# Two-layer cross-attention: stacked operands and row maxima sent to the score matmuls in another order and further ahead

## What is computed

```python
q = hidden @ Wq + bq; k = ctx @ Wk + bk; v = ctx @ Wv + bv      # 256 -> 256, 64, 64
scores = einsum('bkgld,bksd->bkgls', q, k) / sqrt(8) + mask     # 8 key heads, groups of 4
out = einsum('bkgls,bksd->bkgld', softmax(scores), v)
x = out @ Wo + bo + hidden
hidden = (x - mean) * rsqrt(var + 1e-6) * gamma + beta          # input of the second layer
```

## Time and profile before

| | us |
|---|---|
| median of 3 runs | 390.87 |
| range of the runs | 389.21 to 392.48 |
| profiled execution | 394.78 |
| its span, first to last instruction | 393.0 |
| mean granted TensorE clock over the span | 0.911 of full speed |

### The profile page before, as it was taken

One profiled execution on the slowest core, in us unless ns is written; L12 is line 12 of the kernel. 1 busy time (PEld: TensorE's weight loads), 2 busy tenths in 40 slices (PEclk: granted clock), 3 DMA queues, 4 the chain that ended last, 5 costly groups with the idle time before them and its releaser, 6 DMA issues.

```text
span 393.0 us, 8003 instructions
## 1 busy us (share of the span) xinstructions
PE 326.8 (83%) x2720; PEld 212.6 (54%) x2720; DVE 252.1 (64%) x530; ACT 216.6 (55%) x496; POOL 228.8 (58%) x447
## 2 busy tenths in 40 slices
PE   5074597897989799998989899897979797978982
PEld 5074475663666566665656566565636564634321
DVE  6452555474768678777878658585847676764532
ACT  2120256374767667776666647473736665653760
POOL 6044437364677757678576737565746566462634
PEclk9666879898999999999999989898979989896997
DMA  6527875455364653334333333424251434340000
GB/s 194 157 58 214 214 203 132 115 167 161 98 161 109 154 143 109 99 108 110 100 99 99 99 98 93 119 82 137 60 144 49 117 92 127 92 114 15 18 28 30
DMA packets 38490, 44.40 MB, mean 113 GB/s; under 512 B 12208, under 2 KB 32560, under 8 KB 36144
## 3 DMA queue, kind: packets, MB, share of 16 engines
q1 hardware_dynamic: 36080, 42.81, 40.3%
q10 hardware_dynamic: 2368, 1.05, 0.9%
HBM read 33.10 MB, written 9.96 MB: 110 GB/s over the span
## 4 chain that ended last, share of the span: by engine, by line
PE 49%; DMA 24%; SPq 11%; issue 8%; POOL 4%; ACT 3%; DVE 1%; POOLq 0%; ACTq 0%
DMA q_stack<-max_parts 15%; PE oT_bank L804 11%; PE t_bank L711 10%; PE s_bank L697 9%; PE o_bank L830 8%; SPq L276 7%; PE qk_bank L723 4%; DMA q_stack<-q_scratch 3%; DMA q_scratch<-q_parts 3%; PE misc_bank L788 2%; SPq L263 2%; PE o_bank L816 1%; PE o_bank L822 1%; DMA k_scratch<-k_parts 1%; DMA k_stack<-k_scratch 1%
## 5 line engine op out<-in xcount | busy, mean ns | idle before, releaser
L554 DVE TENSOR_REDUCE row_max<-s_bank 128x4 f32<-128x512 f32 x256 | 170.0, 683 | 113.5 <-PE s_bank L697 113.0
L463 ACT ACTIVATE probs<-t_bank 128x512 f32<-128x512 f32 x256 | 152.7, 603 | 121.7 <-PE t_bank L711 119.8
L697 PE MATMUL s_bank<-k_stack,q_stack 72*128 72x128 bf16 x1024 | 104.2, 227 | 38.7 <-DMA k_stack<-k_scratch 18.0
L697 PEld LDWEIGHTS s_bank<-k_stack,q_stack 72*128 72x128 bf16 x1024 | 78.1, 101 | 87.1 <-issue 35.0
L711 PE MATMUL t_bank<-q_stack,k_stack 75*128 75x512 bf16 x256 | 101.5, 399 | 14.1 <-DMA q_stack<-max_parts 12.9
L804 PE MATMUL oT_bank<-probs,v_ones 128*32 128x512 f32 x512 | 79.5, 639 | 0.0
L354 POOL TENSOR_TENSOR q_rest<-qT,q_parts 128x256 f32<-128x256 f32 (+1 forms) x32 | 21.3, 665 | 52.9 <-ACT q_parts L476 43.8
L376 POOL CAST max_parts<-max_neg 96x128 bf16<-96x128 f32 x32 | 9.2, 287 | 53.8 <-DVE max_neg L561 53.6
L830 PE MATMUL o_bank<-wo_sb,attnT 128*128 128x256 f32 x128 | 39.2, 436 | 0.8 <-ACT attnT L498 0.7
L723 PE MATMUL qk_bank<-xT_sb,wq_sb 128*128 128x128 f32 x240 | 39.0, 287 | 0.0
L723 PEld LDWEIGHTS qk_bank<-xT_sb,wq_sb 128*128 128x128 f32 x240 | 38.1, 205 | 1.4
(11 more groups left out here) (81 smaller groups left out, 377.3 us busy)
## 6 DMA issues: line engine op xcount, KB each, us to landing
q_stack<-q_scratch SPq DMA_DIRECT2D x32, 576.0 KB
q_scratch<-q_parts SPq DMA_DIRECT2D x32, 192.0 KB, 2.1
k_stack<-k_scratch SPq DMA_DIRECT2D x96, 48.0 KB
result<-x_sb SPq DMA_DIRECT2D x16, 128.0 KB, 3.8
k_scratch<-k_parts SPq DMA_DIRECT2D x16, 96.0 KB, 3.7
xT_sb<-x_t SPq DMA_DIRECT2D x3, 512.0 KB, 4.8
mask_sb<-mask ACTq DMA_DIRECT2D x2, 512.0 KB, 7.9
cT_sb<-c_t SPq DMA_DIRECT2D x2, 512.0 KB, 5.2
```

Of the source, the lines that this page charges most:

```text
L463: nc.scalar.activation(probs[:, u % 2, kv], t_bank[kv % 2][:], ACT.Exp).then_inc(exp_done, 1)
L554: nc.vector.tensor_reduce(row_max[:, u % 2, GROUP * kv:GROUP * (kv + 1)], s_bank[kv % 2][:].rearrange("p (g s) -> p g s", g=GROUP), AX.X, ...
L697: mm = nc.tensor.matmul(s_bank[kv % 2][:, g * S:(g + 1) * S], q_stack[0:TERM_ROWS, r, GROUP * kv + g], k_stack[0:TERM_ROWS, r, kv], start= ...
```

## The change

- Queries are projected three units ahead (AHEAD = 3) instead of two; the third unit's queries, keys and values are projected in the head.
- The stacks have five places. SyncE's phase t begins with load_max(t-1); load_q and the keys follow for unit t+2 instead of t+1. `load_k` becomes `load_keys(engine, u)`; units 0 and 1 are issued by ScalarE, in its head.
- The context has a ring of 8 places instead of 16 own ones, and its loads wait for the projections of what they overwrite; the ring of key parts has 4 places instead of 8.
- In SyncE's head, store_q(0) and store_k(0) come ahead of the second pieces of x and context. VectorE's head tests the mask before it copies values. K_PLAN and V_PLAN begin with sequence 3.

The core of the diff (semaphore counts that follow from AHEAD, and the moved values, are left out):

```diff
-RING, KEY_RING, PARTS_RING = 4, 3, 8
+RING, KEY_RING, PARTS_RING, CONTEXT_RING = 5, 3, 4, 8
+AHEAD = 3
-CONTEXT_LOADS = (((0, 1), None), ((1, 2), None), ((2, 4), None), ((4, 6), 0), ((6, 8), 1), ((8, 12), 2), ((12, 16), 5))
-X_T_LOADS = (((0, 1), None), ((1, 2), None), ((2, 4), None), ((4, 8), 1), ((8, 12), 4), ((12, 16), 7))
+CONTEXT_LOADS = (((0, 1), None), ((1, 3), None), ((3, 5), None), ((5, 8), None), ((8, 12), 1), ((12, 16), 4))
+X_T_LOADS = (((0, 1), None), ((1, 3), None), ((3, 5), None), ((5, 9), 0), ((9, 13), 4), ((13, 16), 8))
...
+        def load_keys(engine, u):
+            b, layer = u % BATCH, u // BATCH
+            if layer == 0:
+                engine.wait_ge(k_stored[b % STORES], 16 * (b // STORES + 1))
...
+            for part in range(PARTS):
+                engine.dma_start(k_stack[part * HD * PARTS:(part + 1) * HD * PARTS, u % RING].rearrange("p h s -> p (h s)"),
+                                 k_scratch[b, :, layer].rearrange("c d n -> d c n")).then_inc(k_loaded, 16)
...
                 load_context(0)
+                store_q(0)
+                store_k(0)
                 load_x_t(1)
                 load_context(1)
...
-                store_q(0)
-                store_k(0)
                 load_q(0)
-                load_k(0)
+                load_x_t(2)
                 load_context(2)
-                load_x_t(2)
                 store_q(1)
                 store_k(1)
+                load_q(1)
+                load_context(3)
+                store_q(2)
+                store_k(2)
 
             def phase(t):
-                if live(t + 1):
-                    load_q(t + 1)
-                    load_k(t + 1)
-
-                for b in keys_of(t - 1):
-                    if b != t + 1:
-                        store_k(b)
+                if live(t - 1):
+                    load_max(t - 1)
+                if live(t + 2):
+                    load_q(t + 2)
+                    load_keys(sp, t + 2)
...
-                if live(t - 1):
-                    load_max(t - 1)
...
-                if live(t + 2):
-                    store_q(t + 2)
+                if live(t + AHEAD):
+                    store_q(t + AHEAD)
                 for b in keys_of(t):
-                    if b == t + 2:
-                        store_k(b)
+                    store_k(b)
...
                 read_k(0, qk_bank)
+                load_keys(act, 0)
                 read_q(1, 0, o_bank)
                 read_q(1, 1, o_bank)
                 read_k(1, oT_bank)
+                read_q(2, 0, qk_bank)
+                read_q(2, 1, qk_bank)
+                read_k(2, t_bank[0])
+                load_keys(act, 1)
...
-                if live(t + 2):
-                    project_q(t + 2, 0)
+                if live(t + AHEAD):
+                    project_q(t + AHEAD, 0)
```

More of the change, by code:

```diff
@@ L85, in projected @@
 def projected(plan, t, slot):
-    return 2 + sum((at, s) < (t, slot) for at, s in plan)
+    return AHEAD + sum((at, s) < (t, slot) for at, s in plan)
 def cross_attention(nc, x, x_t, c_t, mask, w_q, w_kv, w_o, b_q, b_k, b_v, rows, out):
@@ L233, in load_context @@
                 (low, high), _ = CONTEXT_LOADS[n]
-                sp.dma_start(cT_sb[:, low:high], c_t.rearrange("p (b k) l -> p b k l", b=BATCH)[:, low:high]
+                first = low % CONTEXT_RING
+                need(sp, k_projected, high - CONTEXT_RING)
+                need(sp, v_projected, high - CONTEXT_RING)
+                sp.dma_start(cT_sb[:, first:first + high - low], c_t.rearrange("p (b k) l -> p b k l", b=BATCH)[:, low:high]
                              ).then_inc(context_loaded[n], 16)
@@ L265, in load_q @@
                              .broadcast_to([PARTS * HD, PARTS, HEADS * L])).then_inc(q_loaded, 16)
[L267 to L277, removed]
             def load_max(u):
@@ L313, in phase @@
                         load_context(n)
+                for n, (_, at) in enumerate(X_T_LOADS):
+                    if at == t:
+                        load_x_t(n)
                 u = t - 5
@@ L433, in head @@
                                                ).then_inc(mask_reduced, 1)
-                split_q(1)
-                split_k(1)
+                for u in range(1, AHEAD):
+                    split_q(u)
+                    split_k(u)
             def phase(t):
@@ L445, in phase @@
                     add_bias(t - 3)
-                if live(t + 2):
[L447 to L450, removed]
+                if live(t + AHEAD):
+                    split_q(t + AHEAD)
+                for b in keys_of(t):
+                    split_k(b)
             head()
@@ L529, in slot @@
                         copy_oT(t - 3)
-                    if kv in (4, 5) and live(t + 2):
-                        read_q(t + 2, kv - 4, qk_bank)
+                    if kv in (4, 5) and live(t + AHEAD):
+                        read_q(t + AHEAD, kv - 4, qk_bank)
                     if kv == 6 and live(t - 3):
@@ L659, in head @@
                 nc.vector.tensor_scalar(no_mask_flag[:], mask_most[:], 0.0, None, ALU.is_equal).then_inc(flag_ready, 1)
+                dve.wait_ge(bv_loaded, 16)
+                dve.wait_ge(v_padded, CLEAR_STEPS)
+                dve.wait_ge(v_projected, AHEAD)
+                for b in range(AHEAD):
+                    values(b, b)
             def phase(t):
@@ L729, in key, with value @@
                 for k in range(KT):
-                    mm = nc.tensor.matmul(bank[:, 0:S], wkv_sb[:, k, 0], cT_sb[:, b, k],
+                    mm = nc.tensor.matmul(bank[:, 0:S], wkv_sb[:, k, 0], cT_sb[:, b % CONTEXT_RING, k],
                                           start=(k == 0), stop=(k == KT - 1))
                 mm.then_inc(k_projected, 1)
-            def value(b, bank):
+            def value(b, place):
+                width = LAYERS * KVD
                 for k in range(KT):
-                    mm = nc.tensor.matmul(bank[:, 0:LAYERS * KVD], cT_sb[:, b, k], wkv_sb[:, k, 1],
-                                          start=(k == 0), stop=(k == KT - 1))
+                    mm = nc.tensor.matmul(misc_bank[:, place * width:(place + 1) * width], cT_sb[:, b % CONTEXT_RING, k],
+                                          wkv_sb[:, k, 1], start=(k == 0 and place == 0), stop=(k == KT - 1),
+                                          skip_group_check=True)
                 mm.then_inc(v_projected, 1)
@@ L777, in project_v @@
                 pe.wait_ge(v_ready, LAYERS * b)
-                value(b, misc_bank)
+                value(b, 0)
             def transpose_max(u):
@@ L849, in head @@
                 key(0, qk_bank)
-                value(0, misc_bank)
+                value(0, 0)
                 pe.wait_ge(x_t_loaded[1], 16)
@@ L855, in head @@
                 key(1, oT_bank)
-                value(1, s_bank[1])
+                value(1, 1)
+                pe.wait_ge(k_read, 2)
+                for n in range(KT):
+                    query(2, n, qk_bank, n == 0)
+                pe.wait_ge(q_read, 2)
+                key(2, t_bank[0])
+                value(2, 2)
             def phase(t, masked):
```

47 lines of the change are left out of this document (22 added, 25 removed).

## The result

The changed kernel takes 341.29 us (median of 4 runs, 340.56 to 341.77), the kernel before 391.31 in the same comparison: a ratio of 0.8725, 95% interval 0.8684 to 0.8767. The profiled execution took 341.28 us, 53.5 less than the one of before.

A forecast was written before the change was run, and what follows sets the result against it. TensorE was taken as nearest to the bound, with 66 us idle in waits that also drop its clock. 394.78 (profiled) - 47.4 (phases 3 to 31) - 2.9 (lead-in) + 3.5 (late splits) = 348.0 us; range 340 to 366.

The forecast's parts named there:

- the steady stretches: Phases 3 to 31: without TensorE's waits and the clock drops they cause, 47.4 us saved, before 3.5 us charged back.
- late splits: Layer 0, seven phases where a key split makes GpSimd late for the maxima: 0.5 us each, +3.5 us.
- the lead-in: Start of the kernel: first maxima's transfer leaves earlier, a stall in phase 3 goes; 2.9 us saved, bounds 0 and 5.
- The waits and the clock drops go together: Phases 3 to 31: TensorE's waits and the clock drops they cause share the gain in about 3 to 2.
- The floors: Phase times without waits: 9.35 us with one projection, 9.85 with both, 8.85 in the second half, then 8.45.
- Phases 30 and 31: Last two phases with scores, no query projection, maximum reductions of 0.69 us per slot: 8.75 us each, 4.9 saved.
- Maxima first: SyncE's phase: the maxima's transfer leaves right after the split and lands in 2.5 us, at most 4.2; it fits.
- Rival 1: Each phase: the maxima still arrive last, 0.6 us more in each of 30 phases, 366 us; chance 0.14.
- Rival 2: Another engine, VectorE or ScalarE, paces the phases once TensorE doesn't stop, 370 us; chance 0.08.
- Rival 3: SyncE's queue: loads leave late behind the split and a slower query store; slower, 408 or 396 us; chance 0.03.
- Rival 4: Loads are limited by bandwidth, not lead, so the waits stay; within 1%, 391 us; chance 0.03.

The follow-up runs named there:

- e8: Changed kernel with GpSimd's split of the maxima moved behind inverse_deviation and add_bias in its phase; 437.42 us.
- e1: Kernel before with only the order changed: the maxima's transfer at the head of SyncE's phase, loads still one unit ahead; 473.99 us, ratio 1.21.
- e2: Changed kernel with the maxima's transfer put back behind the phase's loads and result store, loads still two units ahead; 397.99 us, ratio 1.020.
- e10: Changed kernel with the query load issued ahead of the maxima's transfer and the keys behind it; 373.95 us.
- e9: Changed kernel without the second half of the output projection's contraction (two of four matmuls), so the output differs; 328.38 us.
- e11: Changed kernel with VectorE's maxima taken over half of the columns, so the output differs; 339.81 us.
- e6: Changed kernel, loads two units ahead, with the maxima's transfer issued by ScalarE ahead of slot 4's query reads instead of by SyncE; 390.77 us.

## Why the prediction was right

348 was forecast, 341.3 measured, inside the range of 340 to 366. The mechanism was the forecast's, the sizes were off in both directions: the steady stretches, forecast at 263.8 us with the 3.5 for late splits, took 254.4, and the lead-in took 2.4 us more than forecast. That the sum came within 7 us owes something to the two errors' opposite signs.

- **The waits and the clock drops go together.** Right. Steady phases have neither, and the forecast of 3.5 us for late splits in layer 0 was hardly needed: from phase 6 on a phase with both projections takes 9.8 us and one with a single one 9.1, whether GpSimd is 1.2 us late or not. It was near, with under 0.5 us to spare (e8).
- **The floors** were 0.2 to 0.3 us a phase too high (9.35 against 9.09 by the windows of max_neg, 8.85 against 8.64). The rows of before that I took for floors weren't clean, as their columns showed: 9.26 us busy of 9.38, and a clock of 0.96 in the 8.87 us. Why the first was busy for 9.26 and not 9.09 stays open. Where I had a clean row (8.48, clock 1.00), I was right to 0.06. Phases 30 and 31 were priced at 8.75 by slots of 0.69, and take 8.2 and 7.8.
- **The lead-in** is the step that failed: 2.9 us forecast, 0.5 measured (59.55 against 60.07), within my bounds of 0 and 5. Its sign failed too: phase 1's scores start at 35.62 and not at 34 to 35, because TensorE waits 1.29 us for unit 1's keys, which ScalarE issued from 28.55 to 30.61. The splits end at 37.2 and the maxima are split at 39.6, as told. But I let their transfer leave with the split and gave SyncE's queue ahead of it no time. The store of unit 2, issued at 28.96 behind unit 1's query load and a context piece, took 6.6 us to land, so load_q(2) left at 35.57, and what follows it kept SyncE until 41.07. load_max(0) left at 41.11, 1.5 us behind the split, with 2.4 MB issued since 35.57 ahead of it, and was used 6.6 us later, where my working had 5.1 (39.6 to 44.7). These two make the 3.0 us by which TensorE is later than forecast (47.70 against 44.7). From the chain of the changed kernel in order of time:

```profile
28.96 6.59 DMA q_scratch<-q_parts
...
41.11 6.54 DMA q_stack<-max_parts
```

- **Maxima first**: landing 2.9 to 3.3 us, not 2.5 (e8). I had taken the end of the DMA traffic for the landing. It had no effect, since 3.2 to 4.0 us are allowed. The stake was larger than I wrote. I worked the two parts out one after the other, and never what either would do without its partner; e1 and e2 show that either alone gives nothing or a loss, because the order makes the loads late and the loads make the maxima late.
- **Rival 1** (late maxima) is what e10 and e2 are; its price of 18 us was low, 33 and 57 were measured. The waits themselves were near it in e10: from phase 3 to 31 TensorE is idle for 19.9 us, and its busy time is 9.4 us longer than in the changed kernel, at a granted clock of 0.98; in e2 the two are 30.5 and 17.0 us, at 0.95. The changed order avoids it by 1 us in layer 1, and by less than 0.5 behind a late key split.
- **Rival 2** fell with e9 and e11. **Rival 3**: its mechanism is there (the query store lands in 3.5 us by the page, against 2.1), and the point from which it decides was not reached. **Rival 4** fell with the result.

## What to carry to other kernels

In this kernel the small transfer on the critical path needed two things: its issue ahead of the bulk in the queue, and the bulk not yet moving; then the bulk had to have a whole stage more of lead, or the order only traded one wait for another. When you ask when a transfer leaves, follow its queue back to what it last waited for: a lead of two units changed nothing about the moment while the store before it stayed where it was. Two waits that end at nearly the same time hide each other, so price a change of one by what the other then becomes.

## What the runs showed of the hardware

The same 24 KB transfer landed in 2.9 to 3.3 us with nothing big ahead (e8), 4.8 us in the phase shown with 576 KB issued 1.2 us ahead in the same queue (e10; 3.8 to 6.4 in others), 5.6 us from another engine's queue with the query load issued 1.7 us ahead (e6), and 6.5 us in the lead-in with 2.4 MB ahead. The Trainium skill says it for the two queues (DMA: Bandwidth & Descriptors, Issuing engines are not separate DMA queues): both run on the same 16 DMA engines; e6 agrees with its 5.6 us. TensorE's granted clock was 0.50, that is 1.2 GHz, for 6 us behind a wait of 1.98 us in e8, and it stayed at 2.4 GHz for 254 us on end in the changed kernel.
